# The shared expert's first down projections: full float32 by tiles, or three rounded products by chunks

## The reference

```python
x = x + jnp.tanh(g_xattn[0]) * xattn(layernorm(x), ctx, ctx, ...)
# the mixture, on xf = layernorm(x), 2048 rows of D = 256
for e in range(16):
    h = silu(xf @ W1[e] + b1[e]) * (xf @ W11[e] + b11[e])      # 512 hidden
    y = y + (h @ W2[e] + b2[e]) * gates[:, e, None]            # top 2 of 16
z = silu(xf @ Ws1 + bs1) * (xf @ Ws11 + bs11) @ Ws2 + bs2      # 1024 hidden
x = x + jnp.tanh(g_ffn[0]) * (y + z)
```

## Time and profile before

| what | us |
|---|---|
| median of 3 runs (568.67 to 572.27) | 571.85 |
| time of the profiled execution | 574.73 |
| its span | 572.6 |
| stage 2 with the first block, from the second group's first up to `up(1, 1)` (190.14 to 260.54) | 70.40 |
| PE busy in it | 65.55 |

### The profile page before, as it was taken

The page is one execution under the profiler, slowest core; times in us unless marked ns, Lnnn a source line. Parts: engine busy times, 40 slices in busy tenths (PEclk is TensorE's granted clock), DMA queues, the critical chain, the costliest instruction groups (busy, mean ns, idle before and its releaser), DMA issues.

```text
span 572.6 us, 12049 instructions
## 1 busy us (share of the span) xinstructions
PE 546.3 (95%) x3290; PEld 440.9 (77%) x3291; DVE 353.6 (62%) x861; ACT 238.5 (42%) x788; POOL 333.2 (58%) x273
## 2 busy tenths in 40 slices
PE   7889999999979999988999999999999999999996
PEld 6556667666758878777888888888888888888785
DVE  5757788787678732345665566555665556435677
ACT  1899999999994201202222122221222212232232
POOL 4689999998863486623364674444444830236550
PEclk8999999999999999999999999999999999999999
DMA  8571001000112144335458777656665210113332
GB/s 284 245 300 64 21 20 38 29 26 20 65 39 103 46 166 174 105 98 185 140 177 293 249 287 259 201 201 211 211 211 201 82 46 29 35 54 107 109 111 73
DMA packets 32899, 76.08 MB, mean 133 GB/s; under 512 B 4961, under 2 KB 21857, under 8 KB 29921
## 3 DMA queue, kind: packets, MB, share of 16 engines
q1 hardware_dynamic: 14960, 52.44, 25.5%
q10 hardware_dynamic: 14832, 14.82, 8.0%
q0 software_dynamic: 3072, 8.39, 4.7%
HBM read 54.93 MB, written 18.61 MB: 128 GB/s over the span
## 4 chain that ended last, share of the span: by engine, by line
PE 80%; DVE 8%; issue 5%; another core or an unknown queue 3%; ACT 2%; POOL 2%; DVEq 0%; ACTq 0%; POOLq 0%
PE mid L749 14%; PE big L730 8%; PE big L731 8%; PE big L732 7%; PE big L517 5%; PE big L653 4%; PE mid L740 4%; PE big L651 3%; PE big L652 3%; PE mid L530 3%; PE work L549 3%; PE last L670 2%; PE work L670 2%; PE last L542 2%
## 5 line engine op out<-in xcount | busy, mean ns | idle before, releaser
L939 ACT ACTIVATE last<-arena 128x512 f32<-128x512 f32 x47 | 28.3, 602 | 183.3 <-DVE arena L1409 183.3
L837 ACT ACTIVATE arena<-big,nmax 128x128 f32<-128x128 f32 x256 | 90.7, 404 | 9.0 <-DVE nmax L1061 8.4
L749 PE MATMUL mid<-dring,arena 128*128 x376 | 88.9, 379 | 0.0
L1409 DVE TENSOR_TENSOR arena<-big,bring 128x512 f32<-128x512 f32 x47 | 32.5, 692 | 87.2 <-PE big L732 87.2
L730 PE MATMUL big<-u_hi,xsT_hi 128*128 x188 | 81.8, 435 | 1.6 <-issue 1.6
L1572 POOL TENSOR_TENSOR u_lo<-arena,u_hi 128x2048 fp32r<-128x2048 f32 x16 | 74.4, 4652 | 1.3
L749 PEld LDWEIGHTS mid<-dring,arena 128*128 128x128 f32 x376 | 67.8, 190 | 7.4
L732 PE MATMUL big<-u_hi,xsT_lo 128*128 x188 | 73.5, 391 | 0.0
L731 PE MATMUL big<-u_lo,xsT_hi 128*128 x188 | 73.4, 390 | 0.0
L1548 POOL TENSOR_TENSOR arena<-arena,rinv 128x1024 f32<-128x1024 f32 (+1 forms) x32 | 58.7, 1834 | 13.3 <-DVE rinv L1069 13.0
L1672 POOL TENSOR_TENSOR pool_mark<-mhalf 128x1 f32<-128x1 f32 x15 | 2.9, 194 | 104.0 <-PE big L732 87.6
(11 more groups left out here) (198 smaller groups left out, 1202.9 us busy)
## 6 DMA issues: line engine op xcount, KB each, us to landing
arena<-up_w_dram SPq DMA_DIRECT2D x16, 1024.0 KB, 7.6
bring<-expert_bias_dram SPq DMA_DIRECT2D x16, 640.0 KB
dring<-down_w_dram SPq DMA_DIRECT2D x18, 512.0 KB
sorted_y<-arena ACTq DMA_DIRECT2D x47, 128.0 KB, 1.7
arena<-sorted_x ACTq DMA_DIRECT2D x43, 128.0 KB, 2.1
sorted_x<-dring SPq DMA_DIRECT2D x3, 1536.0 KB, 9.4
arena<-ctx_t_dram ACTq DMA_DIRECT2D x8, 256.0 KB, 2.8
dring<-up_w_dram SPq DMA_DIRECT2D x2, 1024.0 KB, 4.8
```

The lines of the kernel that those rows point to most:

```text
L749: i = mm(mid[:, 1, 0:D], gT[:, p, c, :], dring[:, slot, c * D:(c + 1) * D], start=(c == 0), stop=(c == HC - 1))
L837: i = nc.scalar.activation(probs[:, u % 2, h, :], big[:, u % 2, h // 4, (h % 4) * CTX:(h % 4 + 1) * CTX], ACT.Exp, bias=nmax[:, u % 2, h:h ...
L1409: v.tensor_tensor(hb1[:, p, :], big[:, p, 0, :], bring[:, slot, 0:HID], ALU.add).then_inc(h1_ready, 1)
```

## The change

- Stage 2's downs become those of stage 4: `shared_down(n)` by chunks, three rounded products of 256 columns for each tile, four banks at once (`first_bank`). They stand on PE two chunks behind their ups, nearly one up and one down in turn.
- ACT gets 16 roundings of a hidden chunk (`round_hidden`), and the rounding of the down weights (`first_d[:, 0]`, 1,024 columns). DVE gets 16 rests (`keep_rest`) and the rest of the down weights (`first_d[:, 1]`).
- The hidden chunks of stage 2 lie in two alternating buffers (`gg`) and no longer in `gshT`, where the rounded parts and the split weights now lie.
- `keep_xfT(LAST)` leaves POOL: ACT does its rounding, DVE its rest.
- The two products of the counts (`totals_ps`, `rank_ps`) go to other columns of the banks `mid`, and the first down waits for `rank_taken`.
- POOL's split of expert 2's weights waits, besides, for the sixteenth rest.
- The first sorted rows are transposed into the banks `big` between the downs of chunks 14 and 15, and `up(0, 0)` and `up(1, 1)` have no downs between them.

```diff
+        with nc.sbuf_tensor("arena", [P, ARENA], F32) as whole:
+            arena = whole
+        first_d = sb("first_d", [P, 2, DCOLS], F32R)
+        first_gs = sb("first_gs", [P, 2, 2, 512], F32R)
+        sb("arena_rest", [P, ARENA - 2 * DCOLS - 4 * 512])
...
+        first_bank = (work, last, mid[:, 0, :], mid[:, 1, :])
+
+        def hidden_chunk(n):
+            return gg[:, n % 2, :] if n < HC * TILES // GROUP else gshT[:, n // HC % 2, n % HC, :]
+
+        def rounded_chunk(n):
+            if n < HC * TILES // GROUP:
+                return first_gs[:, 0, n % 2, :], first_gs[:, 1, n % 2, :]
+            return gs_hi[:, n % 2, :], gs_lo[:, n % 2, :]
...
-                slot = (ITEMS - 1) % WSLOTS if s >= TILES // GROUP else 0
-                for t in tiles:
-                    n = GROUP * s + t
-                    if n >= 2:
-                        pe.wait_ge(z_taken, n - 1)
-                    for c in range(HC):
-                        if t == 0:
-                            pe.wait_ge(gsh_ready, HC * s + c + 1)
-                        i = mm(zbank[t % 2][:, 0:D], gshT[:, s % 2, c, t * P:(t + 1) * P], dring[:, slot, c * D:(c + 1) * D],
-                               start=(c == 0), stop=(c == HC - 1))
-                    i.then_inc(z_ps, 1)
+            def shared_down(n):
+                h, c = divmod(n, HC)
+                second = h >= TILES // GROUP
+                banks = last_bank if second else first_bank
+                hi, lo = rounded_chunk(n)
+                d = (d_hi, d_lo) if second else (first_d[:, 0, :], first_d[:, 1, :])
+                pe.wait_ge(gs_lo_ready, n + 1)
+                if n == 0:
+                    pe.wait_ge(d_split, 1)
+                    pe.wait_ge(lg_taken, PAIRS)
+                    pe.wait_ge(rank_taken, 1)
+                if n == HC * TILES // GROUP:
...
+                for t in range(GROUP):
+                    if c == 0 and h > 0:
+                        pe.wait_ge(z_taken, GROUP * (h - 1) + t + 1)
+                    g_hi, g_lo = hi[:, t * P:(t + 1) * P], lo[:, t * P:(t + 1) * P]
+                    w_hi, w_lo = d[0][:, c * D:(c + 1) * D], d[1][:, c * D:(c + 1) * D]
+                    mm(banks[t][:, 0:D], g_hi, w_hi, start=(c == 0), stop=False)
+                    mm(banks[t][:, 0:D], g_hi, w_lo, start=False, stop=False)
+                    i = mm(banks[t][:, 0:D], g_lo, w_hi, start=False, stop=(c == HC - 1))
+                    if c == HC - 1:
+                        i.then_inc(z_ps, 1)
+                    elif t == GROUP - 1:
+                        i.then_inc(gs_used, 1)
...
-            mm(mid[:, 1, 0:E], const[:, C_ONE:C_ONE + P], run[:, 0, PAD + TILES - 1, :], start=True, stop=True).then_inc(totals_ps, 1)
-            mm(mid[:, 0, 0:E], const[:, C_TRI:C_TRI + P], run[:, 0, PAD + TILES - 1, :], start=True, stop=True).then_inc(rank_ps, 1)
+            mm(mid[:, 1, D:D + E], const[:, C_ONE:C_ONE + P], run[:, 0, PAD + TILES - 1, :], start=True, stop=True).then_inc(totals_ps, 1)
+            mm(mid[:, 0, D:D + E], const[:, C_TRI:C_TRI + P], run[:, 0, PAD + TILES - 1, :], start=True, stop=True).then_inc(rank_ps, 1)
             shared_up(0, 3)
+            shared_down(0)
             pe.wait_ge(xfT_kept, 4)
-            shared_up(1, 0)
-            shared_up(1, 1)
-            shared_up(1, 2)
-            shared_up(1, 3)
-            pe.wait_ge(w_even, 32)
-            shared_down(0)
+            for n in range(4, 8):
+                shared_up(1, n - 4)
+                shared_down(n - 3)
+            shared_down(5)
             pe.wait_ge(xfT_kept, PAIRS)
-            shared_ups(2)
-            shared_down(1)
-            shared_ups(3)
-            shared_down(2)
+            for n in range(8, 15):
+                shared_up(n // HC, n % HC)
+                shared_down(n - 2)

...
-            transpose_rows(0, 0)
-            shared_down(3, range(1))
-            transpose_rows(1, 1)
+            shared_up(3, 3)
+            shared_down(13)
+            shared_down(14)
+            transpose_rows(0, 0, big[:, 0, 0, :])
+            transpose_rows(1, 1, big[:, 0, 1, :])
+            shared_down(15)
+            pe.wait_ge(xsT_ready, 2)
+            pe.wait_ge(gsh_ready, HC * TILES // GROUP)
             up(0, 0)
-            pe.wait_ge(xsT_ready, 2)
-            shared_down(3, range(1, GROUP))
-            pe.wait_ge(z_taken, 4 * GROUP)
+            pe.wait_ge(z_taken, TILES)
...
+            shared_silu(0, 0)
+            act.wait_ge(w_even, 32)
+            nc.scalar.activation(first_d[:, 0, :], dring[:, 0, :], ACT.Copy).then_inc(d_hi_done, 1)
+            round_hidden(0)
+            act.wait_ge(xfT_ready, PAIRS)
+            nc.scalar.activation(xfT_hi[:, :, 2 * P * LAST:2 * P * PAIRS], xfT[:, :, :], ACT.Copy).then_inc(xfT_hi_kept, 1)
+            shared_silu(0, 1)
+            round_hidden(1)
+            shared_silu(0, 2)
+            for n in range(3, 8):
+                shared_silu(n // HC, n % HC)
+                round_hidden(n - 1)
+            round_hidden(7)
+            for n in range(8, 16):
+                shared_silu(n // HC, n % HC)
+                round_hidden(n)
...
+                    if n >= 2:
+                        dve.wait_ge(gs_lo_ready, n - 1)
+                    v.scalar_tensor_tensor(out=hidden_chunk(n), in0=big[:, c % 2, 1, :], scalar=bias[:, o:o + 1],
...
+            def keep_rest(n):
+                hi, lo = rounded_chunk(n)
+                dve.wait_ge(gs_hi_ready, n + 1)
+                v.tensor_tensor(lo, hidden_chunk(n), hi, ALU.subtract).then_inc(gs_lo_ready, 1)
...
+            keep_rest(0)
+            dve.wait_ge(d_hi_done, 1)
+            v.tensor_tensor(first_d[:, 1, :], dring[:, 0, :], first_d[:, 0, :], ALU.subtract).then_inc(d_split, 1)
...
+            keep_rest(1)
             shared_hidden(0, [3])
+            keep_rest(2)
+            dve.wait_ge(xfT_hi_kept, PAIRS)
+            v.tensor_tensor(xfT_lo[:, :, 2 * P * LAST:2 * P * PAIRS], xfT[:, :, :], xfT_hi[:, :, 2 * P * LAST:2 * P * PAIRS],
+                            ALU.subtract).then_inc(xfT_kept, 1)
             shared_hidden(1, [0])
+            keep_rest(3)
...
+            shared_hidden(1, [1])
+            keep_rest(4)
+            next_lo(1)
+            next_lo(2)
+            shared_hidden(1, [2])
+            next_lo(3).then_inc(split_done, 1)
             dve.wait_ge(w_even, 32)
             add_shared(0)
-            shared_hidden(2, range(HC))
-            add_shared(1)
-            shared_hidden(3, range(HC))
-            add_shared(2)
-            copy_rows(0, 0)
-            add_shared(3, range(1))
-            copy_rows(1, 1)
+            keep_rest(5)
+            shared_hidden(1, [3])
+            keep_rest(6)
+            keep_rest(7)
+            for n in range(8, 15):
+                shared_hidden(n // HC, [n % HC])
+                if n % HC == 1:
+                    add_shared(n // HC - 1)
+                keep_rest(n)
+            shared_hidden(3, [3])
+            keep_rest(15)
+            copy_rows(0, 0, big[:, 0, 0, :])
+            copy_rows(1, 1, big[:, 0, 1, :])
+            add_shared(3)
...
-            add_shared(3, range(1, GROUP))
...
-                if t == GROUP - 1:
-                    keep_xfT(LAST)
                 if t % GROUP == GROUP - 1:
                     pool.wait_ge(scattered, 16 * TOPK * (t + 1))
...
             pool.wait_ge(split_done, 2)
+            pool.wait_ge(gs_lo_ready, TILES)
             split(PIECES, raw[:, 0, :], 0, 0, 1)
```

More of the change, by code:

```diff
@@ L354, in chunk_used @@
             if c == HC - 1:
-                engine.wait_ge(z_ps, TILES + GROUP * (h + 1))
+                engine.wait_ge(z_ps, GROUP * (h + 1))
             else:
@@ L655, in shared_up @@
                     i.then_inc(sh_ps, 1)
[L657 to L672 removed]
+            def shared_down(n):
[10 more added lines that the diff above has]
+                if n == HC * TILES // GROUP:
+                    pe.wait_ge(d_split, 2)
+                    pe.wait_ge(g_ready, BLOCKS)
+                    pe.wait_ge(xsT_ready, BLOCKS)
+                    pe.wait_ge(gT_ready, BLOCKS)
+                    pe.wait_ge(y_ready, BLOCKS)
+                for t in range(GROUP):
[10 more added lines that the diff above has]
+                        i.then_inc(gs_used, 1)
@@ L752, in _ @@
             pe.wait_ge(table_ready, 1)
-            pe.wait_ge(rank_taken, 1)
-            pe.wait_ge(z_taken, 3 * GROUP)
             def slot(n, q, rows, ahead):
@@ L925, in shared_silu, with round_hidden @@
                     .then_inc(silu_ready, 1)
-            for s in range(4):
-                for c in range(HC):
-                    shared_silu(s, c)
+            def round_hidden(n):
+                act.wait_ge(gsh_ready, n + 1)
+                if n >= 2:
+                    chunk_used(act, n - 2)
+                nc.scalar.activation(rounded_chunk(n)[0], hidden_chunk(n), ACT.Copy).then_inc(gs_hi_ready, 1)
+            shared_silu(0, 0)
```

(9 more changed lines are left out.)

76 lines of the change are left out of this document (17 added, 59 removed).

## The result

The changed kernel took 573.84 us (median of 20 runs, 570.64 to 581.16), the kernel before 571.44 beside it (20 runs, 568.12 to 573.21): ratio 1.0041, 95% interval 1.0024 to 1.0059. That is slower by 0.4%, within the 1% that I called no change, and 10 us above my forecast. Runs more than 1.5% above the fastest of their kernel, here the one of 581.16, stand in the medians and are left out of the ratios. Of the others, seven show a mean granted clock of 0.991 to 0.993 and took 575.4 to 576.6 us; of the eleven at 0.996 and up, ten took 570.6 to 573.4. The profiled run took 572.40 us (span 570.6).

The account below looks back on a forecast made before the run. PE was taken as the bound, busy for 95% of the span. `up(1, 1)` 8.5 us earlier, less 0.4 for contention, gave 8.1 us: 571.85 - 8.1 = 563.7 us, range 560.5 to 568.0.

Parts of the forecast that it names:

- The downs themselves: Stage 2's downs on PE: rounded products take 23.0 us instead of 26.8, a gain of 3.8 us.
- The larger gain: Rival: the kernel gains more than the forecast of 561.7 to 565.7 us; chance 0.08.
- The rank: Before the first down, DVE's added work delays `rank_taken` by some 1.1 us, so PE waits 0.9 us.
- The scatter: Scatter and row loads: only 0.2 us later, loads issued at 240.7 instead of 240.5, with 2.2 us cover.
- First rows: Ahead of `up(0, 0)`: PE waits 0.5 us for the rows, with the start gap of 0.72 inside that wait.
- the gap of 0.85: PE's idle time ahead of `up(1, 1)`, expected to stay, with that up at 252.0 instead of 260.54.
- The chunks: PE's alternating ups and downs, 4.18 us a chunk: narrowest at chunk 5, 0.6 us cover, no stall taken.
- I take 0: The size given to PE's waits for rests in the chain of chunks: none, 0 us.
- the chain by chunks stalls PE: Rival: two or three near chunks 4 to 6, where DVE makes the block table, cost 2 to 4 us; chance 0.11.
- Contention: DVE against POOL: 0 us on the scatter, 0.4 us on PE from gate instructions inside POOL's split.
- my 8.5 us: Up to `up(1, 1)`: it starts 8.5 us earlier, 3.8 from the products, 4.7 from idle time and starts.

Follow-up runs that it names:

- plain chunks: Changed kernel's order by chunks with plain float32 downs in stage 2 and POOL's split not waiting for the sixteenth rest; median 2.7 us under the kernel before.
- sessions 1 to 3: The first three of five groups of follow-up runs, each sharing one timing of the kernel before (567.22 us in session 1); no late silus with the full scatter.
- early_gates: Changed kernel with the gates' exp and four DVE gate instructions moved from behind `add_shared(3)` to ahead of hidden chunk 8; 562.26 us.
- before_again: The kernel before, unchanged, run again for a profile on the same chip as the changed kernel; `up(1, 1)` at 68.53 us from the end of `shared_up(0, 3)`.
- after_again: The changed kernel, unchanged, run once more, without late signals; `up(1, 1)` at 61.81 us and third up at 67.91 from the end of `shared_up(0, 3)`.
- session 4: Fourth group of follow-up runs, on another chip than sessions 1 and 5, with late signals; the kernel before took 569.28 us.
- session 5: Fifth group of follow-up runs, on the chip of session 1 but with late signals; the kernel before took 573.09 us.
- half_scatter_again: Changed kernel with the last 16 of 32 scatters left out, in session 5; 565.76 us against 573.96 for the changed kernel.
- half_scatter_after: Changed kernel with the last 16 of 32 scatters left out, in session 1; 0.5% faster than the kernel before.
- gates_hoisted: Changed kernel with gates ahead of hidden chunk 8 and PE's two waits ahead of `up(0, 0)` behind its register loads; session 4, fastest run 561.62 us.
- after_third: The changed kernel, unchanged, run a third time on another chip; its fourth up starts 5.0 us behind the third.

## Why the prediction was wrong, by its steps

*The downs themselves*: right. Twelve matmuls take 1.43 us, and plain chunks are 3.6 us longer up to `up(1, 1)`; I had 3.8. The larger gain, to which I gave 0.08, needs a rounded product well under the 120 ns of stage 4; no run shows one, and in stage 2 it takes 1.43 / 12 = 119 ns. *The rank*: I had a wait of 0.9, it is 0.63. *The scatter* lost nothing, its row loads were issued at 240.34 (I had 240.7). *First rows*: the idle time ahead of `up(0, 0)` is 1.6 us, not 0.5, because the start gap is not inside the wait but behind it; the gap of 0.85 that I had kept ahead of `up(1, 1)` is gone in return. Without late signals `up(1, 1)` starts 61.81 us behind the end of `shared_up(0, 3)`; I had 252.0, and the trace of before has that end at 190.30, so 61.7.

**The step that failed is "The chunks", with its "I take 0".** The sum let a silu start when its up ends. That holds in all eleven profiles of sessions 1 to 3 and not in the one at hand: of chunks 8 to 13 each came 2.8 to 7.5 us late, PE stopped, and `up(1, 1)` started at 69.00 instead of 61.81, 7.2 us later. My rival "the chain by chunks stalls PE" named the right chain and a wrong place and cause: chunks 4 to 6, DVE busy. What it missed was in the trace of before: silus that wait for "remote". The kernel before loses to late signals as well, 1.7 us in this stretch (70.24 against 68.53), which I had counted as idle time to be gained. So at best 6.8 of my 8.5 us were there, and 6.7 came (68.53 less 61.81).

**The second failure is a term mis-sized: what the gates cost in "Contention".** I had 0.4 us for all of it. From `up(1, 1)` to the third up 2.7 us go back, 1.84 of them by the gates (early_gates); the rest I put down to the first block's chain, which has lost its cover, and no run took that alone. The 0.4 was an estimate, that the last gate, a product of two SBUF tensors, waits for POOL's end. No run shows that: it took 0.17 to 0.22 us in all twenty traces, and in none did it fall inside this split. What waited was the first, with one SBUF input: 2.90 us inside the split, up to its end, and 0.18 outside it (plain_chunks). What decides between the two outcomes at 242.8 us was not shown.

So without late signals: 8.5 - 1.7 - 2.7 = 4.1 us at the third up (measured 71.95 - 67.91 = 4.0), and 3 to 4.3 us in the median (0.9946, 0.9943). With them, the changed order has nothing behind an up that hides its silu but one down and one up, and loses 6 to 10 us (570.39 and 573.96 against 563.9) where the kernel before loses 2 to 6 (569.28 and 573.09 against 567.3). Part of it is the clock: seven of the first twenty runs.

Two more differences bear on the sum. The profiled run of before, whose rows the prediction used, had late signals in its last stage as well, silus up to 3.2 us late beside POOL's gather: from the third up to its end it takes 308.7 us, before_again 304.8. The wait of 2.1 us in the earlier trace rows, the ground of a rival, is not in before_again. And the changed kernel takes 305.7 us for that part in after_again, so that 0.9 of the 4.0 us are lost behind the third up; where, was not looked for.

**What stays open.** Why PE's signals are late in some runs: what else happens on the chip at such a time was not seen. Whether the matmuls that PE issues in a microsecond matter: session 4 speaks for it (2.2 against 7.1 us), session 5 against it (6.9 against 7.3), with one profile each.

One rival is untested and strong: the recording itself. Every time here comes with a recording of the run, and the kept traces differ in it. From 190 to 242 us, the scatter, the eight traces with late silus and a full scatter hold 232 to 291 semaphore records, and the nine without late silus 696 to 724. From 490 us on, the gather, it is 820 to 875 against 1,227 to 1,272. Between and before they hold nearly the same. With half the scatter it is 304 in half_scatter_again and 507 in half_scatter_after. (For the changed kernel in all: 5,445, 5,435 and 5,449 records with late signals, 6,318 and 6,319 without.) So signals are late exactly in the traces that lose records, and in the two stretches where they lose them. Whether one causes the other, or both come of a third thing, no run shows; if it is the recording, a run without one would not lose this time.

## What to carry to other kernels

A sum of durations takes each wait to end when its cause does; look first whether the trace of before bears that out, start against end, wherever the new order will have less slack, and count what it shows as lost, not as idle time to be won. Look where a DVE instruction that is moved will start inside a long one of POOL: the first gate, 0.18 us on its own, lasted to the end of POOL's subtraction (2.90 us), and the rest that began together with it took 0.69 or 5.07 us. An order with more work of PE behind each up (plain chunks) kept its gain when the signals came late; one that was 0.7 us faster without them lost it. That it was the slack is argued: plain chunks also had the earlier split, and in one session less late signals. And a trace that lacks semaphore records which another of the same kernel has is a warning that its late signals may not be the program's.

## What the runs showed of the hardware

- While GpSimd's indirect DMAs run, PE's signals can come late, at some times and not at others on the same chip (567.22 and 573.09 us for the same kernel): for ScalarE up to 7.5 us, and for VectorE too (in gates_hoisted `add_shared`, line 1336, has 1.3 us of waits for "remote"). The recorded increments of ScalarE, VectorE and GpSimd stood within 0.01 us of their instruction's end from 176 to 262 us in all twenty traces. None comes later than 7.5 us in the eight profiles that have them at full scatter. The same traces lack some 14% of the semaphore records that the others of the same kernel have (5,445 against 6,318), so the recording may take part.
- A VectorE instruction of 16 columns with one SBUF input took 2.90 us inside a GpSimd subtraction and 0.18 us outside it (plain_chunks). One of 512 columns that began with it took 0.69 or 5.07 us.
- A start made 1.1 us earlier made the kernel 1.6 us slower: the wait behind it grew to 2.5 us, PE's granted clock was 0.50 from 256 to 262 us, and the fourth up followed the third 2.8 us later than in after_third (7.8 against 5.0).
